# A graph-attention kernel, layer 0: mask gathers beside value gathers, weighted sums spread between them, prefix and maximum moved in order and in memory

## The reference

```python
h = jnp.maximum(_layernorm(x, axis=-1), 0.0)
Whs, Wht, Whc = h @ Ws, h @ Wt, h @ Wc          # 64, 64 and 128 columns
e = jnp.einsum('nh,mh->nm', Whs, Wht)
z = jnp.where(adj > 0, e, NEG)                   # adj is int32, 8192 x 8192
x = x + softmax(z, axis=-1) @ Whc
...
x = x + elu(attention of layer 1 over the same adj)
```

## Time and profile before

| | us |
|---|---|
| median of three runs | 1359.65 |
| the profiled execution | 1364.51 |
| its span, first to last instruction | 1362.7 |
| TensorE busy in the span | 1270.7 (93%) |
| VectorE busy | 1043.8 (77%) |
| ScalarE busy | 980.1 (72%) |
| weighted sums, line 787, busy | 246.6 |
| one evacuation of a mask bank by ScalarE (line 1126) | 0.597 |
| one make_pick on VectorE (line 1477) | 2.292 |

### The profile page before, as it was taken

How to read it: one execution, slowest core, us unless ns; L and a number is a source line. 1 busy time by engine, 2 the same in 40 slices (tenths; PEclk the granted TensorE clock), 3 DMA queues, 4 the chain that set the end, 5 groups by cost and what they waited for, 6 DMA issues and landing times.

```text
span 1362.7 us, 74732 instructions
## 1 busy us (share of the span) xinstructions
PE 1270.7 (93%) x31691; PEld 1125.0 (83%) x31691; DVE 1043.8 (77%) x2196; ACT 980.1 (72%) x2100; POOL 165.8 (12%) x331
## 2 busy tenths in 40 slices
PE   4868899999999999999999999988899999999996
PEld 3657788888888888888888888876899989999996
DVE  6846467767776766777777677657899989999997
ACT  4855466666666666666666666667898989999995
POOL 4210111111111111111111111012000000000000
PEclk9969899999999999999999999999899999999998
DMA  9773699999999999999999999610234334334332
GB/s 188 77 89 67 91 127 138 139 138 129 140 140 131 133 137 133 136 137 141 129 138 141 140 126 139 108 48 2 73 111 117 100 102 127 108 100 126 112 96 73
DMA packets 103503, 157.54 MB, mean 116 GB/s; under 512 B 11456, under 2 KB 36288, under 8 KB 102848
## 3 DMA queue, kind: packets, MB, share of 16 engines
q0 software_dynamic: 36864, 67.13, 52.4%
q1 hardware_dynamic: 66496, 88.37, 20.0%
HBM read 314.84 MB, written 41.94 MB: 262 GB/s over the span
## 4 chain that ended last, share of the span: by engine, by line
PE 76%; issue 9%; ACT 8%; DVE 4%; DMA 2%; POOL 1%; ACTq 0%; SPq 0%; DVEq 0%; POOLq 0%
PE ps L883 16%; PE ps L787 16%; PE ps L734 10%; PE ps L857 9%; PE ps L766 6%; PE ps L749 4%; PE ps L761 4%; PE ps L722 4%; ACT arena L1117 3%; ACT arena L1126 3%; PE ps L775 1%; DMA arena<-in_adjB 1%; PE ps L663 1%; PE ps L639 1%; PE ps L880 1%
## 5 line engine op out<-in xcount | busy, mean ns | idle before, releaser
L787 PE MATMUL ps<-arena 128*128 128x129 f32 x2048 | 246.6, 279 | 0.0
L883 PE MATMUL ps<-arena 128*128 128x129 f32 x2048 | 244.9, 278 | 0.7 <-issue 0.7
L1133 ACT ACTIVATE arena<-ps,neg_max 128x1024 f32<-128x1024 f32 x128 | 142.3, 1112 | 135.5 <-PE ps L787 135.5
L787 PEld LDWEIGHTS ps<-arena 128*128 128x128 f32 x2048 | 237.8, 194 | 0.0
L883 PEld LDWEIGHTS ps<-arena 128*128 128x128 f32 x2048 | 236.7, 194 | 0.9 <-issue 0.9
L1486 DVE TENSOR_REDUCE mx<-ps 128x1 f32<-128x1024 f32 x128 | 156.7, 1225 | 97.1 <-PE ps L766 92.7
L1117 ACT ACTIVATE arena<-ps 128x512 f32<-128x512 f32 x256 | 152.6, 596 | 100.9 <-PE ps L734 100.9
L589 POOL DMA_DIRECT2D arena<-in_adjB x256 | 136.6, 534 | 688.2 <-PE ps L749 672.6
L1691 DVE TENSOR_SCALAR arena<-arena 128x128 f32<-128x128 f32 x768 | 202.6, 341 | 15.0 <-issue 8.6
L1111 ACT ACTIVATE arena<-ps 128x512 f16<-128x512 f32 x256 | 153.6, 600 | 41.2 <-PE ps L722 38.6
L734 PE MATMUL ps<-arena 128*32 128x128 f16 x8192 | 164.7, 222 | 19.0 <-issue 9.3
(11 more groups left out here) (164 smaller groups left out, 1321.8 us busy)
## 6 DMA issues: line engine op xcount, KB each, us to landing
arena<-in_adjB POOLq DMA_DIRECT2D x256, 256.0 KB, 8.1
sel_pick<-arena SPq DMA_DIRECT2D x64, 256.0 KB, 6.2
sel<-arena SPq DMA_DIRECT2D x64, 256.0 KB, 6.2
arena<-sel_pick SPq DMA_DIRECT2D x64, 256.0 KB, 3.5
arena<-sel SPq DMA_DIRECT2D x64, 256.0 KB, 2.7
arena<-in_xB SPq DMA_DIRECT2D x4, 1024.0 KB, 6.0
x_t<-in_x SPq DMA_DIRECT2D x64, 64.0 KB, 5.0
x_mid<-arena SPq DMA_DIRECT2D x64, 64.0 KB, 5.1
```

Source lines behind the costliest of these rows:

```text
L787: last = nc.tensor.matmul(pv_ps, p_T[:, s * P:(s + 1) * P], v_sel[:, b, s, :], start=False, stop=(s == SB - 1), skip_group_check=True)
L883: last = nc.tensor.matmul(xv_ps[b], w_msk[:, b, s, :], x1_sel[:, b, s, 0:VW], start=False, stop=(s == SB - 1), skip_group_check=True)
```

## The change

In layer 0's steps:

- Bank 6 takes the transposed maximum too: `mx_ps` moves from bank 7, which it shared with the weighted sums, into the last quarter of bank 6, the bank of the mask gathers, where the prefix already was.
- On TensorE the mask group 1 of tile a moves from the end of the step before to the start of step i, mask groups 2 and 3 stand later, the prefix and the transposition stand between weighted sums 0 and 1, and the four groups of weighted sums are spread over the step. Scores 0 and 1 stand together.
- The waits follow: the prefix and the transposition wait until ScalarE has emptied mask group 1 of tile a; mask group 2 waits until VectorE has read both (`posx_ready`, `top_done`); the transposition and the weighted sums no longer wait for one another's bank.
- ScalarE's evacuations and exponentials are put into the matching order.
- On VectorE `spread_maximum(c)` stands behind `indicate(e, 1)` and no longer ahead of it.

```diff
-        mx_ps = ps[:, 7, 256:256 + P]
+        mx_ps = ps[:, 6, 3 * P:4 * P]
...
                 if dst is pre_ps:
-                    wait(pe, m_evac, t * 4)
+                    wait(pe, m_evac, t * 4 - 2)
...
                 wait(pe, m_evac, t * 4 + q)
+                if q == 2:
+                    pe.wait_ge(posx_ready, min(t + 2, TILES) if isinstance(t, int) else t + 2)
+                    wait(pe, top_done, t)
...
                 pe.wait_ge(mx_ready, t + 1)
-                wait(pe, y_ready, t - 1)
+                pe.wait_ge(m_evac, min(t * 4 + 6, TILES * 4) if isinstance(t, int) else t * 4 + 6)
...
                     wait(pe, y_ready, t)
-                    pe.wait_ge(top_done, min(t + 2, TILES) if isinstance(t, int) else t + 2)
...
                 if there(i, 3):
                     scores(c, cb, 3)
+                if there(i, 2):
+                    pick_mask(a, b, 1)
+                if there(i, 3):
                     pick_values(c, cb, 2)
                 if there(i, 2):
-                    pick_mask(a, b, 2)
                     pick_keys(a, b, 1)
+                if there(i, 4):
+                    weigh(d, b, 0)
+                if within(i, EARLY + 1, TILES + 1):
+                    prefix(e, pre_ps)
+                if there(i, 3):
+                    turn_maximum(c)
+                if there(i, 4):
+                    weigh(d, b, 1)
                 if there(i, 3):
                     pick_values(c, cb, 3)
                 if there(i, 2):
+                    pick_mask(a, b, 2)
+                    pick_keys(a, b, 2)
+                if there(i, 4):
+                    weigh(d, b, 2)
+                if there(i, 2):
                     pick_mask(a, b, 3)
-                if there(i, 3):
-                    turn_maximum(c)
-                if there(i, 2):
-                    pick_keys(a, b, 2)
                     pick_values(a, b, 0)
-                if within(i, EARLY + 1, TILES + 1):
-                    prefix(e, pre_ps)
                 if there(i, 4):
-                    for g in range(4):
-                        weigh(d, b, g)
+                    weigh(d, b, 3)
                 if there(i, 2):
                     pick_keys(a, b, 3)
                     scores(a, b, 0)
+                    scores(a, b, 1)
                     pick_values(a, b, 1)
                 if there(i, 1):
                     pick_mask(e, cb, 0)
-                if there(i, 2):
-                    scores(a, b, 1)
-                if there(i, 1):
                     pick_keys(e, cb, 0)
-                    pick_mask(e, cb, 1)
                 if there(i, 2):
                     scores(a, b, 2)
...
             def tile_step(i, b):
                 e, a, c, cb = i - 1, i - 2, i - 3, 1 - b
+                if there(i, 2):
+                    take_mask(a, b, 1)
                 if there(i, 3):
                     take_values(c, cb, 2)
                 if there(i, 2):
-                    take_mask(a, b, 2)
                     take_keys(a, 1)
                 if there(i, 3):
                     take_values(c, cb, 3)
                 if there(i, 2):
-                    take_mask(a, b, 3)
-                    take_keys(a, 2)
+                    take_mask(a, b, 2)
                 if there(i, 3):
                     exps(c, 0)
                 if there(i, 2):
+                    take_keys(a, 2)
+                    take_mask(a, b, 3)
                     take_values(a, b, 0)
                     take_keys(a, 3)
...
-                if there(i, 3):
-                    spread_maximum(c)
                 if within(i, EARLY + 1, TILES + 1):
                     indicate(e, 1 - b, 1)
                 if there(i, 3):
+                    spread_maximum(c)
                     maximum(c)
```

More of the change, by code:

```diff
@@ L1160, in tile_step @@
                     take_keys(e, 0)
-                    take_mask(e, cb, 1)
             first_preparation()
```

## The result

The changed kernel took 1465.21 us (median of three runs, 1458.72 to 1466.92) against 1359.65: a ratio of 1.077 (95% interval 1.073 to 1.082), 105.6 us slower. The forecast was 1412, and its range ended at 1440. The direction was right and the size was half of what came. Times further down are medians too; the four runs of the kernel with the selection stored later lay between 1421.4 and 1442.8 us, and the longest, the profiled one, counts as slow, being 1.5% above the shortest, and is left out of the median.

A forecast was written before the change was run, and what follows sets the result against it. TensorE was taken to bound layer 0 at 12.50 us a step; a late fourth mask load would make it 13.4, so 0.9 us x 58 steps = 52 us on 1359.65 gives 1412 us, range 1361 to 1440.

The forecast's parts named there:

- The two stalls: TensorE's two short waits per step behind ScalarE's evacuation of the one-bank buffer (values, masks): 0.22 us each, removed.
- The ring through VectorE: Scores 3 (S3) to transposition of the maximum (T) 3.76 us, back to S3 8.74: a 12.50 us step, gain taken back.
- W at 0.91 us a piece: On TensorE, each group of weighted sums (W) takes 0.91 us, from 3.62 for four in a row.
- much slower rival: Weight loads show at each weighted-sums piece on TensorE, stores cost their full 1.84 us: step 13.9, kernel 1441 us; chance 0.08.
- The spread behind the indication: On VectorE the maximum's spread comes 1.24 us further back, so TensorE's transposition of the maximum waits 0.6 to 0.7 us.
- Load 3 is allowed 3.7 us later: Fourth mask load, issued 4.05 us after the maximum's transposition, is late for VectorE's second indication by 0.85 to 0.9 us.
- One landing for all steps: In the mask-load queue, load 3 lands 11.6 us after the maximum's transposition, worked out with the queue empty before load 2.
- The price of 1.6 for the stores: SyncE's stores fall inside the fourth mask load's window and delay it by 0.8 to 1.84 us, taken as 1.6.
- I price the pause at nothing for the clock: TensorE's new pause of some 1.5 us a step costs nothing in granted clock, 0.979 on average before.
- The ring that the forecast names: Mask group 3, mask load 3, VectorE's second indication, transposition of the maximum: a ring of 13.4 us a step.
- the one in which the loads stay hidden: Rival: mask loads land in time and VectorE's ring sets the step, 12.5 to 12.55 us; kernel 1360 to 1363; chance 0.12.
- The faster one: Rival: loads in time, TensorE's way from transposition to scores 3 under 8.74 us; step 12.3, kernel 1348 us; chance 0.10.

The follow-up runs named there:

- the last experiment: Kernel before the change, with mask group 1 behind scores 2 and scores 3 moved from the next step's start to behind it: 1342.5 us.

## Why the prediction was right or wrong

By its own steps:

- **The two stalls go: right.** The changed kernel shows neither. And the last experiment puts one of them at some 0.20 us a step, close to the 0.22 read in the earlier trace rows.
- **The ring through VectorE is 12.50 us: too short by 0.25.** Stripped of the loads it is 12.75 on average, and in the step shown 3.82 from S3 to T (forecast 3.76) and 8.97 from T to S3 (forecast 8.74). The term that failed is W at 0.91 us a piece, taken from four in a row. The forecast has 0.99, 0.99 and 0.91 for the three pieces behind T, with the changes of 0.08 that it adds to two of them; they take 1.03, 1.07 and 1.00, 0.21 more, which is nearly all of the 0.23. The forecast had this only in its much slower rival. Against the kernel before this ring costs 11 us over the 54 steps; with the loads it enters through the issue of load 3, since two such pieces stand between T and mask group 3.
- **The spread behind the indication makes T wait 0.6 to 0.7 us: right for the move by itself** (0.6 measured in the old order). In the new order it is beside the point, since the prefix needs the threshold at the same place.
- **Load 3 is allowed 3.7 us later, is late, and closes a ring: right.** It is what decides: with small loads nine tenths of the loss go, load 3's landing is followed by the next T after 1.9 us in all 54 steps (forecast 1.80), and a late load 3 in the old order costs 65 to 113 us. By the step shown it was right even in size: issue at T + 4.29 (forecast 4.05), landing at T + 11.6 (11.6), step 13.53 (13.4). Part of that is luck. The forecast takes the queue to be empty when load 2 is issued, yet by its own numbers loads 0 and 1 are done 16 us after T, that is 3.5 after the next T, and load 2 goes at 2.3. In the step shown load 1 landed 1.53 us after the issue of load 2, and in 50 of the 54 steps it was still under way then. Load 2 was issued at T + 2.46, took 5.4 us for the 5.0 of an empty queue and landed at T + 7.8, not 7.3 to 7.5, and load 3 followed 3.8 us later, where the forecast has 4.2 (on the mean it is 4.3). The page of the Trainium skill weighed in the prediction ("DMA: Bandwidth & Descriptors", Anatomy of one DMA) gives 4.4 us for such a load, an estimate; the trace disagrees the more, and the row was the better source.
- **One landing for all steps: wrong.** The forecast worked out a single step, from a queue that is empty again each time. The shown step is near it, but even with a clock that falls only once the mean is 13.99 (the kernel with the pause filled). Over the 54 steps of the changed kernel load 3 took 6.6 to 9.8 us to land, 7.86 on the mean, where the forecast has 7.55 for each. VectorE waited 1.14 us a step, not 0.85 to 0.9. The price of 1.6 for the stores fits the gap between the landings of loads 2 and 3 (4.3 us, and 2.7 with the stores moved), and still only 28 us came back, since the stores then met the next loads: it is no term that can be taken away from the sum alone. What remains open is why the landings vary. That a queue which is asked for during nearly the whole of a step cannot make up a hole fits its share, down from 89.2 to 81.9%, and the run with earlier mask groups, in which load 3 is issued 1.0 us earlier and lands no earlier; but this was argued and not shown by itself.
- **"I price the pause at nothing for the clock": wrong.** TensorE's pauses ahead of the prefix, 1.70 us a step, made the granted clock fall in some 16 places of the loop, behind pauses of 1.5 to 3.7 us, and filling them gave back 19 us by the medians, 0.44 us a step in the profiled executions. This term had no place in any case of the forecast, its much slower rival included, and so the range ended too low.

The ring that the forecast names, term by term, with the means over the 54 steps (us; the first three from T):

| | load 3 issued | it takes | it lands | from there to T | step |
|---|---|---|---|---|---|
| forecast | 4.05 | 7.55 | 11.6 | 1.80 | 13.4 |
| after | 4.68 | 7.86 | 12.54 | 1.89 | 14.43 |
| after, pause filled | 4.27 | 7.83 | 12.10 | 1.89 | 13.99 |
| after, selection stored later | 4.62 | 7.27 | 11.89 | 2.04 | 13.93 |
| after, mask groups 2, 3 earlier | 3.71 | 8.83 | 12.54 | 1.97 | 14.51 |

So 0.63 of the missing 1.03 us lie in the issue of load 3, 0.31 in its landing and 0.09 behind it. The clock enters through the first: with the pause filled the issue is 0.41 us earlier and the landing takes as long as before. The forecast's step is 0.9 us longer than the old one, the measured one 1.88. The prediction named the mechanism and the place, and missed half of the size in terms that all lay on the same side.

Of the rivals, the one in which the loads stay hidden (1360 to 1363 us) has the time of the kernel with small loads, 1363.3, but by luck: there the step is 12.75 and not 12.5 to 12.55, and what small loads gain ahead of the steady steps hides that. The faster one fell: even with small loads, the order costs 0.20 us a step.

## What to carry to other kernels

When the transfers of a loop need nearly all of a step, ask for each of them when it is *allowed*, not how long it takes: here a reordering of computation that frees a buffer a third of a step later costs more than the stalls it removes, and the wait it causes is then paid again, through the transfers of the next step and through TensorE's clock. Price a new pause of TensorE with the clock at both levels, even if it is only a microsecond or two long, and take the length of a piece from rows where the work stands in such pieces. Do not take one landing for all: look at what is still under way when a load is issued, in a row of steps. If one stall is the aim, move as little as possible: the mask group alone gave nothing, because a pause at the loop's jump took its place, and with scores 3 it gave 17 us, where the large reordering lost 106.

## What the runs showed of the hardware

- TensorE's granted clock fell to 0.50 behind pauses of 1.2 to 1.4 us in steps of 14 us (the old order with load 3 held to scores 1), in some 12 steps and not in the others, whose pauses are as long. In the changed kernel 1.5 us of needless products in the pause kept it at 1.00 from 200 to 800 us and made the kernel 19 us faster.
- A jump of the loop showed as a pause of 0.45 us on TensorE when a mask group of 0.33 us stood directly ahead of it (steps of 12.83 and 12.26 us in turn), as 0.12 us in the kernel before, where scores 2 stand there (12.58 and 12.46), and not at all with mask group 1 and scores 3 there. Two orders that differ only in the side of the jump on which scores 3 stand are 18 us apart.
- A mask load of 256 KB landed 5.0 us after its issue in the kernel before at 128.08 us, with no other load under way, and 4.9 to 5.2 us after it in all 42 steps between 200 and 800 us of the kernel with load 3 held to scores 1. It took 5.4 in the changed kernel's step shown, where the load ahead of it landed 1.5 us after its issue. The one behind it, issued 1.83 us later, landed 3.8 us after it; in the kernel before, two loads issued 2.35 us apart landed 2.55 us apart.
